# Self-attention scores in a fused decoder layer: matmuls of 256 moving columns become matmuls of 128

## The reference

```python
starts = jnp.arange(num_windows) * (W // 2)      # W = 64
idx = starts[:, None] + jnp.arange(W)
qw, kw, vw = q[:, :, idx, :], k[:, :, idx, :], v[:, :, idx, :]
qg = qw.reshape(B, R, G, num_windows, W, D)
scores = jnp.einsum('brgnqd,bgnkd->brgnqk', qg, kw) * scale
attn = jax.nn.softmax(scores, axis=-1)
og = jnp.einsum('brgnqk,bgnkd->brgnqd', attn, vw)
o = o.transpose(0, 2, 3, 1, 4).reshape(B, num_windows * W, H * D)[:, :L, :]
```

## Time and profile before

| | |
|---|---|
| median of 3 runs | 2553.73 us (2553.38 to 2555.62) |
| the profiled execution, its own time | 2555.84 us |
| its span in the profile | 2554.2 us |
| mean granted TensorE clock | 0.985 |
| TensorE busy over the span | 2430.3 us, 95% |
| VectorE, ScalarE, GpSimd busy | 1695.3, 1303.2, 1192.0 us |

### The profile page before, as it was taken

The page is one execution under the profiler, slowest core; times in us unless marked ns, Lnnn a source line. Parts: engine busy times, 40 slices in busy tenths (PEclk is TensorE's granted clock), DMA queues, the critical chain, the costliest instruction groups (busy, mean ns, idle before and its releaser), DMA issues. The chain is left out here.

```text
span 2554.2 us, 45759 instructions
## 1 busy us (share of the span) xinstructions
PE 2430.3 (95%) x14878; PEld 2210.8 (87%) x14878; DVE 1695.3 (66%) x4773; ACT 1303.2 (51%) x3307; POOL 1192.0 (47%) x1577
## 2 busy tenths in 40 slices
PE   6999999799999999999999989999999999999698
PEld 5888888689998998999898979999999999999586
DVE  6777777475656657575656666665757575767776
ACT  5666776364545545454545455454545454545411
POOL 4766777253434434343433344343535353435554
PEclk9999999899999999999999999999999999999899
DMA  3454447211111112121122111111111111123243
GB/s 115 156 167 133 162 156 254 79 58 57 43 53 60 58 43 64 42 64 53 39 90 76 58 63 58 43 53 40 57 58 60 48 48 57 39 72 115 90 150 122
DMA packets 101476, 207.69 MB, mean 81 GB/s; under 512 B 20048, under 2 KB 49456, under 8 KB 101152
## 3 DMA queue, kind: packets, MB, share of 16 engines
q1 hardware_dynamic: 95680, 186.78, 22.8%
q0 software_dynamic: 5600, 18.41, 2.2%
HBM read 139.83 MB, written 65.32 MB: 80 GB/s over the span
## 5 line engine op out<-in xcount | busy, mean ns | idle before, releaser
L1383 POOL TENSOR_SCALAR x_probs<-x_probs,x_inv 112x376 f32<-112x376 f32 x512 | 634.8, 1249 | 190.7 <-DVE x_inv L1583 190.7
L1377 POOL TENSOR_SCALAR x_bias<-x_top 112x1 f32<-112x1 f32 x512 | 124.1, 242 | 904.7 <-DVE x_top L1555 904.4
L1439 ACT ACTIVATE x_probs<-x_probs,x_bias 112x376 f32<-112x376 f32 x512 | 308.5, 603 | 421.0 <-POOL x_bias L1377 421.0
L1698 PE MATMUL x_ps_r<-x_wo,x_oT 128*128 128x512 f32 x1344 | 345.1, 392 | 1.4 <-DVE x_wo L1481 1.4
L1684 PE MATMUL x_ps_f<-x_xT,x_wq 128*128 128x448 f32 x1536 | 339.1, 370 | 2.5 <-DVE x_v L1526 2.0
L1644 PEld LDWEIGHTS x_ps_o<-x_pT,x_v 128*128 128x128 f32 (+1 forms) x2304 | 294.5, 191 | 34.1 <-DVE x_pT L1562 15.5
L1644 PE MATMUL x_ps_s<-x_kT,x_qT 128*112 128x376 f32 x1536 | 312.9, 339 | 3.9 <-DVE x_top L1555 3.9
L1644 PE MATMUL x_ps_f<-ctxT,x_wk 128*128 128x376 f32 x1536 | 307.9, 336 | 8.0 <-POOL x_ident L45 5.7
L1644 PE MATMUL x_ps_o<-x_pT,x_v 128*128 128x224 f32 (+1 forms) x2304 | 299.1, 274 | 10.6 <-DVE x_pT L1562 10.6
L1644 PE MATMUL x_ps_f<-x_wv,ctxT 128*128 128x512 f32 (+1 forms) x1152 | 304.4, 401 | 4.7 <-DVE x_kT L1526 4.6
L1684 PEld LDWEIGHTS x_ps_f<-x_xT,x_wq 128*128 128x128 f32 x1536 | 280.6, 188 | 30.4 <-DVE x_v L1526 8.7
(11 more groups left out here) (224 smaller groups left out, 3984.3 us busy)
## 6 DMA issues: line engine op xcount, KB each, us to landing
ctxT<-ctxs SPq DMA_DIRECT2D x62, 752.0 KB
ctxs<-ctxT SPq DMA_DIRECT2D x32, 752.0 KB, 5.4
x_xT<-h2T SPq DMA_DIRECT2D x15, 896.0 KB
room<-in_ctx_dram SPq DMA_DIRECT2D x32, 256.0 KB
experts<-in_L_ffn_W_dram SPq DMA_DIRECT2D x32, 256.0 KB, 4.5
w_xa<-in_x_dram SPq DMA_DIRECT2D x32, 224.0 KB, 5.1
w_xr<-in_x_dram SPq DMA_DIRECT2D x32, 224.0 KB, 4.6
x<-w_xr SPq DMA_DIRECT2D x32, 224.0 KB, 5.2
```

The costliest lines, as they stand in the source:

```text
L1377: pool.tensor_scalar(bias[:, m:m + 1], top[:, m:m + 1], -0.1 * NEG, -SCALE, ALU.max, ALU.mult) \
L1383: pool.tensor_scalar(probs[0:T, m, 0:SE], probs[0:T, m, 0:SE], inv[:, m:m + 1], None, ALU.mult).then_inc(normed, 1)
L1439: act.activation(probs[0:T, m, 0:SE], probs[0:T, m, 0:SE], ACT.Exp, bias=bias[:, m:m + 1], scale=SCALE, accum_out=total[:, m:m + 1]).then_ ...
L1698: last = pe.matmul(ps_r[:], oT[:, a, h, slot:slot + P], wo[:, b_, h, :], start=h == 0 and (a, b_) == PASSES[0], stop=h == H - 1 and (a, b_ ...
```

## The change

Each of `qa` and `qb` now holds both windows: `qa` window 0 in partitions 0 to 63 (two heads) and window 1 in partitions 64 to 127 (the other two), `qb` the other way round. `kd` is 128 columns wide: a row group has its keys in column block j % 2, and its window slot is chosen by row group, so that slot 0 holds window 0's keys in the upper row groups and window 1's in the lower. In a score matmul, rows 0 to 63 of the output (window 0) then take two heads and rows 64 to 111 (window 1) the other two. For each `m` there are two accumulations of three matmuls over 128 columns, into neighbouring parts of the bank, so the matmuls stay 24 a batch. The heads stand in another order in the lower rows, which `A` undoes by its index `(q + w) % 2`.

A Q fill is copied in four passes of 64 partitions on each engine. K's copies on ScalarE stay four and each of the first three raises `keys_hi`; VectorE's eight low passes (`low_keys`) now go row group by row group, each pair behind its own copy. The zero parts of `qa` and `qb` are cleared by eight memsets, each of 64 partitions.

```diff
--- before.py
+++ after.py
@@ -207,7 +207,7 @@
         h2 = sb("h2", [P, 2, C])
         qa = sb("qa", [P, 2, KC, TB, T], F32R)
         qb = sb("qb", [P, 2, KC, TB, T], F32R)
-        kd = sb("kd", [P, 2, TB, 2, 4 * WIN], F32R)
+        kd = sb("kd", [P, 2, TB, 2, 2 * WIN], F32R)
         vt = sb("vt", [WIN, 2, TB, 2, WIN])
         vd = sb("vd", [P, 2, TB, 2, 2, P], F32R)
         probs = sb("probs", [P, 2, HEADS // 2, WIN])
@@ -245,7 +245,7 @@
         scores_ready, top_ready, less_ready, exp_ready = sem("scores"), sem("top"), sem("less"), sem("exp")
         total_ready, inv_ready, normed = sem("total"), sem("inv"), sem("normed")
         probsT_ready, p_raw, pT_lo = sem("probsT"), sem("p_raw"), sem("pT_lo")
-        biased = sem("biased")
+        biased, keys_hi = sem("biased"), sem("keys_hi")
         fill_ready, fill_hi, fill_done = sem("fill_ready"), sem("fill_hi"), sem("fill_done")
         ctx_padded, ctx_in, ctx_ready, ctx_raw, ctx_lo = (sem("ctx_padded"), sem("ctx_in"), sem("ctx_ready"),
                                                           sem("ctx_raw"), sem("ctx_lo"))
@@ -541,12 +541,15 @@
                 if kind == "K":
                     src = b[:, 0:TB * KT].rearrange("p (b t) -> p b t", b=TB)
                     return [(src[D * j:D * (j + 1), :, 32 * w:32 * w + WIN],
-                             *[kd[D * j:D * (j + 1), a, :, w, WIN * j:WIN * (j + 1)] for a in (HI, LO)],
-                             bks[D * j:D * (j + 1), :]) for w in range(2) for j in range(4)]
+                             *[kd[D * j:D * (j + 1), a, :, (w + j // 2) % 2, WIN * (j % 2):WIN * (j % 2 + 1)]
+                               for a in (HI, LO)],
+                             bks[D * j:D * (j + 1), :]) for j in range(4) for w in range(2)]
                 if kind == "Q":
                     src = b[:, 0:TB * QT].rearrange("p (b t) -> p b t", b=TB)
-                    return [(src[:, :, 0:R0], *[qa[:, a, n, :, 0:R0] for a in (HI, LO)], bqs[:, n:n + 1]),
-                            (src[:, :, WIN // 2:QT], *[qb[:, a, n, :, R0:T] for a in (HI, LO)], bqs[:, n:n + 1])]
+                    tokens = ((0, R0, 0), (R0, T, WIN // 2))
+                    return [(src[h * WIN:(h + 1) * WIN, :, at:at + hi - lo],
+                             *[q[h * WIN:(h + 1) * WIN, a, n, :, lo:hi] for a in (HI, LO)], bqs[h * WIN:(h + 1) * WIN, n:n + 1])
+                            for k, q in enumerate((qa, qb)) for h in range(2) for lo, hi, at in [tokens[(h + k) % 2]]]
                 if kind == "W":
                     src = b[:, 0:TB * WIN].rearrange("p (b t) -> p b t", b=TB)
                     return [(twice(src[WIN * g:WIN * (g + 1), :, D * g:D * (g + 1)], 0),
@@ -563,11 +566,12 @@
 
             @block.scalar
             def _(act):
-                def both_windows(b, j):
-
-                    w0 = b[D * j:D * (j + 1), 0:TB * KT].rearrange("p (b t) -> p b t", b=TB)[:, :, 0:WIN]
-                    parts, batches, keys = w0.ap
-                    return bass.AP(tensor=w0.tensor, offset=w0.offset, ap=[parts, batches, [WIN // 2, 2], keys])
+                def both_windows(b, j, first):
+
+                    at = WIN // 2 * first
+                    w = b[D * j:D * (j + 1), 0:TB * KT].rearrange("p (b t) -> p b t", b=TB)[:, :, at:at + WIN]
+                    parts, batches, keys = w.ap
+                    return bass.AP(tensor=w.tensor, offset=w.offset, ap=[parts, batches, [WIN // 2 - 2 * at, 2], keys])
 
                 def fill(turn, f):
                     b = ps_f[fills.bank(turn, f)]
@@ -581,8 +585,11 @@
                         act.wait_ge(h2_out[((f[1] - 3) % TB) // 2], turn.count(16, 0) if f[1] == 3 else turn.count(16, -16))
                     if f[0] == "K":
                         for j in range(4):
-                            last = act.activation(kd[D * j:D * (j + 1), HI, :, :, WIN * j:WIN * (j + 1)], both_windows(b, j),
+                            last = act.activation(kd[D * j:D * (j + 1), HI, :, :, WIN * (j % 2):WIN * (j % 2 + 1)],
+                                                  both_windows(b, j, j // 2),
                                                   ACT.Identity, bias=bks[D * j:D * (j + 1), :])
+                            if j < 3:
+                                last.then_inc(keys_hi, 1)
                         last.then_inc(fill_hi, 1)
                         return
                     for src, hi, lo, bias in places(f, b):
@@ -719,8 +726,9 @@
                 dve.memset(power[:], -0.5).then_inc(power_ready, 1)
 
                 for a in (HI, LO):
-                    dve.memset(qa[:, a, :, :, R0:T].bitcast(F32), 0.0)
-                    last = dve.memset(qb[:, a, :, :, 0:R0].bitcast(F32), 0.0)
+                    for k, q in enumerate((qa, qb)):
+                        dve.memset(q[k * WIN:(k + 1) * WIN, a, :, :, R0:T].bitcast(F32), 0.0)
+                        last = dve.memset(q[(1 - k) * WIN:(2 - k) * WIN, a, :, :, 0:R0].bitcast(F32), 0.0)
                 last.then_inc(zeroed, 1)
 
                 def split(n, what):
@@ -748,6 +756,9 @@
 
                 def fill(turn, f):
                     b = ps_f[fills.bank(turn, f)]
+                    if f[0] == "K":
+                        low_keys(turn, f, b)
+                        return
                     dve.wait_ge(fill_hi, fills.until(turn, f, HALVED))
                     if f[0] == "M":
 
@@ -765,6 +776,18 @@
                         else:
                             last = dve.scalar_tensor_tensor(out=lo, in0=src, scalar=bias, in1=hi.bitcast(F32),
                                                             op0=ALU.add, op1=ALU.subtract)
+                    last.then_inc(fill_done, 1)
+
+                def low_keys(turn, f, b):
+
+                    for n, (src, hi, lo, bias) in enumerate(places(f, b)):
+                        if n == 6:
+                            dve.wait_ge(fill_hi, fills.until(turn, f, HALVED))
+                        elif n % 2 == 0:
+                            at = Turn(turn.at + 1, turn.reg)
+                            dve.wait_ge(keys_hi, at.count(3, n // 2 + 1))
+                        last = dve.scalar_tensor_tensor(out=lo, in0=src, scalar=bias, in1=hi.bitcast(F32),
+                                                        op0=ALU.add, op1=ALU.subtract)
                     last.then_inc(fill_done, 1)
 
                 def less_top(turn, s):
@@ -907,7 +930,7 @@
                         for w, (lo, hi) in enumerate(((0, R0), (R0, T))):
                             last = product(rows[:, :, lo:hi],
                                            [(vd[:, a, s, w, q, :],
-                                             pT[:, b_].rearrange("p (c q) t -> p q c t", q=2)[:, q, :, lo:hi])
+                                             pT[:, b_].rearrange("p (c q) t -> p q c t", q=2)[:, (q + w) % 2, :, lo:hi])
                                             for q in range(2) for a, b_ in PASSES])
                     else:
                         at, s = back(turn, n, 2)
@@ -930,9 +953,10 @@
 
                             pe.wait_ge(less_ready, turn.count(8, 2 * s + u - 1))
                         for m in range(2 * u, 2 * u + 2):
-                            last = product(ps_s[u][0:T, (m % 2) * 4 * WIN:(m % 2 + 1) * 4 * WIN],
-                                           [(q[:, a, m, s, :], kd[:, b_, s, w, :])
-                                            for w, q in enumerate((qa, qb)) for a, b_ in PASSES])
+                            for k, q in enumerate((qa, qb)):
+                                at = (m % 2 * 2 + k) * 2 * WIN
+                                last = product(ps_s[u][0:T, at:at + 2 * WIN],
+                                               [(q[:, a, m, s, :], kd[:, b_, s, k, :]) for a, b_ in PASSES])
                         last.then_inc(scores_ready, 1)
 
                 def context(turn, s):
```

## The result

The changed kernel takes 2592.36 us (median of 4 runs, 2591.04 to 2594.11), the kernel before 2553.89 (4 runs, 2553.38 to 2555.62): 1.015 times as long, 95% interval 1.0132 to 1.0167. That is +38.5 us where +32.7 was forecast, and inside the range. The profiled execution took 2591.28, its span is 2589.5.

A forecast was written before the change was run, and what follows sets the result against it. TensorE, busy 408.64 of the first 460 us, was taken as nearly the bound. Scores -11.2, queries +14.2, clock +26 and start +3.7 summed to +32.7 us, 2586.4 us on the median scale; range 2557 to 2602.

The forecast's parts named there:

- Scores: Score matmuls on TensorE: 98 ns instead of 118 from start to start, counting in three steps of four; -11.2 us.
- The bound by the load: Score matmuls on TensorE: 97 ns if the load alone sets the price and shrinks with its columns.
- Queries: Q fills on ScalarE and VectorE: four passes without overlap, 1.83 us a Q; first scores 1.77 us later, eight places; +14.2 us.
- Keys: VectorE's early low key passes: TensorE's 1.27 us wait before Q2 goes but moves before the scores; worth nothing.
- Clock: TensorE behind a 3.6 us wait: 0.50 clock for 8.4 us on average, 3.7 us lost in seven regular turns; +26 us.
- The first turn: TensorE's first turn: already has its 0.50 clock, beside a 4.09 us wait that hides more of it; no clock loss.
- Start: Clearing qa and qb at the start: eight memsets instead of four, each as long; +3.7 us, or 0 if input came late.
- Sum: Whole kernel: -11.2 + 14.2 + 26 + 3.7 = +32.7 us, 2586.4 us on the scale of the medians.
- the clock did not hold: Rival on TensorE's clock: it holds, everything else as forecast; +6.7 us, 2560.4 us; chance 0.15.
- the passes did not overlap: Rival on the Q passes: they overlap after all, 1.41 us a Q; -9.1 us, 2544.6 us; chance 0.10.
- the narrow matmuls did save: Rival on score matmuls: narrow ones save nothing, still 118 ns by the load alone; +43.9 us, 2597.6 us; chance 0.07.

The follow-up runs named there:

- run 9: The kernel of 7, each score matmul after the first batch streaming only 128 of its 256 key columns, the rest left out; 2527.1 us, ratio 0.989.
- 7: The kernel before, with the early low key passes and a separate wait for each Q fill; scores stay 256 columns wide; 2536.94 us, ratio 0.9933.
- run 4: The changed kernel, with 15 unread matmuls of 512 columns filling TensorE's wait before a turn's first scores; 2563.08 us, ratio 1.003.
- run 10: The kernel of 7, each score matmul after the first batch streaming only 64 of its 256 key columns, the rest left out; 2527.92 us, ratio 0.9897.
- Run 1: The kernel before, with only each Q fill copied in four 64-partition passes, alternating upper, lower, upper, lower; scores stay 256 columns wide; 2587.82 us, ratio 1.0122.
- run 2: The kernel before, with each Q fill in four 64-partition passes, both of the upper half first, then both of the lower; 2571.76 us, ratio 1.0059.
- run 3: The kernel before, with only the change's early low key passes, each pair behind its own copy, kd staying wide; 2543.69 us, ratio 0.9953.
- run 6: The changed kernel, with the low halves of qa and qb cleared by two GpSimd memsets, only the high halves on VectorE; 2586.35 us, ratio 1.0125.
- run 5: The changed kernel, with the first scores of a turn waiting for each Q fill on its own, not for the last of four; 2565.82 us, ratio 1.005.

## Why the prediction was right

**Scores, -11.2 forecast.** 98 ns was measured, the value taken. By themselves narrow matmuls gave -9.8 us (run 9 against 7). In the changed kernel they gave somewhat more: in run 4 a turn takes 53.30 - 52.88 = 0.42 us longer though its scores start 1.95 later, so the rest of it became 1.5 shorter, 12 us in eight turns. The bound by the load, which I had inferred from one row at 224 columns, is borne out by run 10 and the row of 8 columns. The figure of 81 ns that the Trainium skill (TensorE: Matmul & The Clock Gate, Back-to-back issue gap) gives for 128 columns does not hold for these operands: 98 was measured.

**Queries, +14.2.** A Q cost 1.84 us on ScalarE against 1.83 worked out, and the scores started 1.95 us later instead of 1.77. In the first turn it was 1.63 (12.19 us behind K's first copy against 10.56): 7 x 1.95 + 1.63 = 15.3. Runs 1 and 2 show both halves of the reason, that a pass does not get shorter with fewer partitions and that a change of the row group takes the overlap away. The rule of the Trainium skill for VectorE (VectorE: DVE Perf Modes, Two Vector instructions with no wait between them) fits the rows shown: K's eight passes take 3.95 us with a change before each and 3.56 where they go in pairs. ScalarE behaves alike: 0.37 us from start to start on one half, 0.42 with a change.

**Keys, nothing.** This step was wrong by little. I had taken ScalarE's chain as if it never waited for TensorE again. Run 1, which has the same slow Q passes and no early keys, shows that it does: 0.36 us behind K. Its first scores start 321.63 - 306.79 = 14.84 us after K's first copy, those of the changed kernel 14.27. So the early keys are worth up to 0.57 us a turn there, not nothing; no run splits this from the other order of the Q passes. What I wrote of the edit with its cover gone, up to 1.27 a turn, was too low: 1.55 was measured, 12 us in all (run 3).

**Clock, +26.** The wait was forecast at 3.6 us and is 4.0; the stretches at 0.50 at 8.4 us on average and are 8.9. Filling the wait (run 4) gives back 29 us of medians, 26.4 of spans, and 57.04 - 53.30 = 3.7 us a turn, the value worked out. This is the largest term. That it came out so close is in part luck: the 8.4 was the middle of two single stretches, and nothing on record said how often each length would come (it was two short and five long). Behind the waits of 3.1 and 2.3 us of runs 1 and 2 the stretches were shorter or missing.

The first turn was taken to lose nothing. That was wrong by little: its clock is at 0.50 for 20.5 us instead of 6.7, and from its first scores to the next K copy it takes 41.44 us where it took 41.65, 0.2 less, when the regular turns with the clock held have 1.5 less. So about 1.3 us were lost there, an estimate from these distances.

**Start, +3.7.** It is 9.13 - 5.02 = 4.1 us to the first statistics, and 4.1 to the first K matmul (23.71 against 19.61; run 6 took 3.9 of them back). The memsets take as long as before and stand further apart, 0.25 us idle before every second one instead of 0.16.

**Sum.** -9.8 + 15.3 + 26.4 (spans of run 4) + 4.1 = +36.0, and 34 with the -12 for the scores, against 2589.5 - 2554.2 = 35.3 of the spans and 38.5 of the medians. Between spans and medians lies the spread of executions: the profiled one of before lies 2.0 over its median, that of after 1.1 under it. The three rivals are out: the clock did not hold, the passes did not overlap, the narrow matmuls did save.

## What to carry to other kernels

Before a matmul is narrowed, ask what its operands then cost the engines that write them: here 10 to 12 us of matmul time was bought with twice the number of copy passes for the queries, and each copy costs by its columns, not its partitions (0.47 us for 64 x 256, 0.48 for 128 x 256). Where passes on several row groups can't be avoided, put those of one group next to each other. A delay of two microseconds at one point of a loop can cost more in granted clock than in waiting (here 26 us against 15): look at the clock behind each new wait, and let the first product of the next stage wait only for the piece that it reads.

## What was unexpected of the hardware

A float32r matmul with a load of 112 columns takes 98 ns from start to start at 64 and at 128 moving columns, 118 at 256, and 187 at 128 columns while the granted clock is 0.50. A product with a load of 128 columns takes 112 ns at 8 moving columns. Two waits of about 1 us with six matmuls between them lowered the clock in some turns of a loop and not in others (run 5), while a wait of 2.3 us did so in two turns of seven (run 2).
